# Degree counts in one run, routing between the gathers, and a rebuilt edge stage and combination in a graph and expert kernel

## The reference, cut to what matters

```python
# 1. relational graph layer
h_all = einsum('nd,rdo->rno', LN(x), W_r)                     # 16 products of every node
deg   = maximum(zeros((16, N)).at[edge_type, dst].add(1), 1)  # edges by relation and destination
msg   = h_all[edge_type, src] / deg[edge_type, dst][:, None]
x     = x + segment_sum(msg, dst) + LN(x) @ W0.T + b0
# 2. eight experts of F = 1024, one for each token, with a capacity
probs = softmax(LN(x) @ gate_w + gate_b); idx = argmax(probs); prb = the chosen probability
pos   = running count of the tokens of that expert - 1;  kept = pos < CAP
buf[idx, pos] = LN(x);  ybuf = relu(buf @ w1 + b1) @ w2 + b2  # each expert
x     = x + nan_to_num(ybuf[idx, pos] * prb * kept, nan=0, posinf=1e4, neginf=-1e4)
# 3. graph convolution with 1/sqrt(degree) at both ends, over the same edges and loops
# 4. an LSTM over the nodes and two running sums
```

## Time and profile before

| | |
|---|---|
| median of three runs | 4495.27 us |
| profiled execution | 4494.84 us, span 4493.1 us |
| granted TensorE clock, mean | 0.879 |
| TensorE busy | 3700.8 us (82%) |
| VectorE busy | 1837.3 us (41%) |
| ScalarE busy | 887.5 us (20%) |
| GpSimd busy | 1631.3 us (36%) |

### The profile page before, as it was taken

How to read it: one execution, slowest core, us unless ns; L and a number is a source line. 1 busy time by engine, 2 the same in 40 slices (tenths; PEclk the granted TensorE clock), 3 DMA queues, 4 the chain that set the end, 5 groups by cost and what they waited for, 6 DMA issues and landing times. The chain is left out here.

```text
span 4493.1 us, 64320 instructions
## 1 busy us (share of the span) xinstructions
PE 3700.8 (82%) x19849; PEld 2830.6 (63%) x19850; DVE 1837.3 (41%) x5512; ACT 887.5 (20%) x2492; POOL 1631.3 (36%) x1753
## 2 busy tenths in 40 slices
PE   3999999988878888865999865656667778999996
PEld 1444454457777777754666644555555557999996
DVE  3444420024334443444222283233344554444687
ACT  0333323310000000023111170000000002444453
POOL 1000000047777777733000036777777770000000
PEclk9999999978787777755999986788888899999998
DMA  4333333333333333332122054344455554433333
GB/s 156 121 120 123 125 116 149 147 117 111 110 110 111 111 111 110 111 122 90 62 82 80 28 158 133 107 126 136 148 152 161 174 183 156 148 111 115 108 108 107
DMA packets 213227, 545.38 MB, mean 121 GB/s; under 512 B 42897, under 2 KB 111358, under 8 KB 198119
## 3 DMA queue, kind: packets, MB, share of 16 engines
q1 hardware_dynamic: 121816, 297.98, 19.7%
q0 software_dynamic: 83344, 235.38, 17.8%
q10 hardware_dynamic: 7808, 8.92, 0.6%
HBM read 363.19 MB, written 178.51 MB: 121 GB/s over the span
## 5 line engine op out<-in xcount | busy, mean ns | idle before, releaser
L731 POOL DMA_INDIRECT a_msg<-scratch_hrel,k_rel_row x784 | 749.7, 956 | 1078.8 <-issue 1072.4
L1519 POOL DMA_INDIRECT b_msg<-scratch_gtab,k_src_row x784 | 763.2, 973 | 269.3 <-issue 263.5
L1568 PE MATMUL b_ps<-b_hit,b_msg 128*128 128x128 f32 x3136 | 492.6, 323 | 304.6 <-DMA b_msg<-scratch_gtab,k_src_row 296.4
L665 PE MATMUL r_psm<-k_w,r_xnT 128*128 128x512 f32 x1568 | 741.6, 609 | 0.9 <-ACT r_xnT L608 0.9
L834 PE MATMUL a_ps<-a_hit,a_msg 128*128 128x128 f32 x3136 | 562.9, 354 | 184.1 <-DMA a_msg<-scratch_hrel,k_rel_row 176.5
L1568 PEld LDWEIGHTS b_ps<-b_hit,b_msg 128*128 128x128 f32 x3136 | 460.9, 233 | 367.2 <-issue 299.6
L834 PEld LDWEIGHTS a_ps<-a_hit,a_msg 128*128 128x128 f32 x3136 | 522.2, 260 | 218.2 <-DVE a_hit L773 141.4
L1946 PE MATMUL l_psg<-k_hall,k_whhT 128*128 128x128 f32 x4672 | 565.8, 279 | 5.7 <-DVE k_hall L2063 5.5
L1946 PEld LDWEIGHTS l_psg<-k_hall,k_whhT 128*128 128x128 f32 x4672 | 542.9, 192 | 13.5 <-DVE k_hall L2063 5.9
L665 PEld LDWEIGHTS r_psm<-k_w,r_xnT 128*128 128x128 f32 x1568 | 278.0, 191 | 273.8 <-issue 251.8
L617 ACT COPY r_hst<-r_psm 128x512 f32<-128x512 f32 x392 | 229.6, 586 | 517.7 <-PE r_psm L665 517.5
(11 more groups left out here) (255 smaller groups left out, 3769.9 us busy)
## 6 DMA issues: line engine op xcount, KB each, us to landing
scratch_hrel<-r_hst SPq DMA_DIRECT2D x98, 1024.0 KB
l_xr<-scratch_xrow SPq DMA_DIRECT2D x146, 512.0 KB, 3.6
scratch_xrow<-n_xs SPq DMA_DIRECT2D x50, 512.0 KB, 3.2
a_msg<-scratch_hrel,k_rel_row POOLq DMA_INDIRECT x784, 2.8
b_msg<-scratch_gtab,k_src_row POOLq DMA_INDIRECT x784, 2.8
scratch_buf<-k_zpad POOLq DMA_DIRECT2D x8, 1024.0 KB, 6.6
scratch_ybuf<-x_ys POOLq DMA_DIRECT2D x8, 1024.0 KB
x_xr<-scratch_buf SPq DMA_DIRECT2D x7, 1024.0 KB, 15.1
```

The source lines that it names most:

```text
L665: mm = pe.matmul(psm[:, c % 4], xnT[:, u, kk], k.w[:, kk, c * 512:(c + 1) * 512], start=(kk == 0), stop=(kk == 1))
L731: pool.indirect_dma_start(msg[:, q, j], None, table, bass.IndirectOffsetOnAxis(ap=rows[:, g, j:j + 1].bitcast(U32), axis=0)).then_inc(s_m[ ...
L1519: pool.indirect_dma_start(msg[:, q, j], None, k.gtab, bass.IndirectOffsetOnAxis(ap=k.src_row[:, g, j:j + 1].bitcast(U32), axis=0)).then_in ...
L1568: mm = pe.matmul(ps[:, u, kk, 0:WIN], msg[:, g % SL, j, kk * P:(kk + 1) * P], hit[:, u, j], start=(j == 0), stop=(j == PER - 1))
```

## The change

The edge stage loads rows 0 to 95 and the 97th row apart, gives each of the three arrays a semaphore, takes W_r's loads behind them on the same queue, lets ScalarE load W0, the bias and the first four tiles of x, turns W0 there, and shares the evictions and memsets out. `Degrees` has buffers for seven groups, and all seven are counted behind chunk 7; the row sums are ten products of the spread counts with a selector of five columns, before the last tile. Gathers and routing become one stage, written out in full as the second gather stage is, with tile work set between groups from the group at which a tile is finished. Tokens are routed in batches of 8 (five), 6 and 3. The gate is written as column 256 of a row of `buf`, which is 264 wide. The experts weigh, clamp and test their outputs themselves and load their first weights at their start. The combination only gathers and adds, with eight and four buffers in place of six and three, and VectorE normalises every even tile.

```diff
@@ class Degrees
-        self.hit = sb("d_hit", [P, 2, PER, WIN], BF16)
+        self.hit = sb("d_hit", [P, BUNCH, PER, WIN], BF16)      # BUNCH = 7, CUTS = 5
+        self.n = k.NP // CUTS
+        self.wide, self.inv = (sb(n, [CUTS * k.R, self.n], F32) for n in ("d_wide", "d_inv"))
+        self.sel = sb("d_sel", [P, 2, CUTS], F32)
@@ count
         pe.wait_ge(self.s_p, 2 * g + 2)
-        pe.wait_ge(self.s_add, g + 1)
+        pe.wait_ge(self.s_add, g - u + BUNCH)
         for j in range(PER):
-            mm = pe.matmul(self.ps[0:self.k.R, u, 0:WIN], self.hot[:, u, j], self.hit[:, u, j],
+            mm = pe.matmul(self.counted(u), self.hot[:, u, j], self.hit[:, u, j],
@@ rows_pe
-        for t in range(k.NP // P):
-            mm = pe.matmul(self.ps[:, 0, t:t + 1], k.degT[:, t * P:(t + 1) * P], k.ones[0:k.R, 0:1],
+        pe.wait_ge(self.s_sel, 3)
+        pe.wait_ge(self.s_go, 16 * CUTS)
+        for t in range(self.n // P):
+            mm = pe.matmul(self.ps[:, 0, t * CUTS:(t + 1) * CUTS], self.wide[:, t * P:(t + 1) * P],
+                           self.sel[0:CUTS * k.R, 1], start=True, stop=True)
@@ stage_relations, vector, counting tiles
-                                for c in range(PT):
-                                    g = (XR * i + s) * PT + c
-                                    q = s * PT + c
-                                    deg.build(v, g + 1, (q + 1) % 2)
-                                    deg.add(v, g, q % 2, None)
+                                adds(XR * i + s)
+                                builds(XR * i + s + 1)
@@ scalar: the root of tile t + 2
-                        if more >= 2:
-                            ln.root(act, t + 2)
...
+                            if c == 6 and more >= 2:
+                                ln.root(act, t + 2)
@@ tensor
                             if c == 3 and more:
                                 turn(t + 1, 1 - u)
-                            if c < len(groups):
-                                deg.count(pe, *groups[c])
+                        for g in groups:
+                            deg.count(pe, *g)
...
-                    if counted:
-                        deg.rows_pe(pe, NG + 2)
                     with pe.Fori(LB, NB) as i:
...
+                    if counted:
+                        deg.rows_pe(pe)
                     tile(NR - 1, 0, False, [])
@@ stage_edges, sync
-                sp.wait_ge(s_fill, 3)
                 for a, v in enumerate((dst, src, etype)):
                     rows = v[0:full * EG].rearrange("(g e) -> g e", e=EG)
-                    sp.dma_start(raw[:, a, 0], rows[0:H]).then_inc(s_ld, 16)
-                    sp.dma_start(raw[0:full - H, a, 1], rows[H:full]).then_inc(s_ld, 16)
+                    sp.dma_start(raw[:, a, 0], rows[0:H]).then_inc(s_ld[a], 16)
+                    sp.dma_start(raw[0:low, a, 1], rows[H:H + low]).then_inc(s_ld[a], 16)   # low = 96
+                    if a == 0:
+                        sp.wait_ge(s_tail, 2)
+                    sp.dma_start(raw[low:full - H, a, 1], rows[H + low:full]).then_inc(s_ld[a], 16)
...
+                    if a == 0:
+                        ...                      # firsts -> base_i, with a semaphore of its own
+                for r in range(k.R):
+                    sp.dma_start(k.w[:, :, r * k.D:(r + 1) * k.D],
+                                 W_r[r].rearrange("(k p) o -> p k o", p=P)).then_inc(k.s_w, 16)
@@ stage_first (in place of stage_gather, weighted, and stage_route), gpsimd
+                    for g in slots:
+                        if along and g < NG:
+                            q = g % SL
+                            if g >= SL:
+                                hold(k, pool, s_mm, g - SL + 1)
+                            for j in range(PER):
+                                pool.indirect_dma_start(msg[:, q, j], None, table, ...).then_inc(s_m[q][j], 16)
+                        for b in ended(g - 10):
+                            scatter(b)
@@ tensor
+                    for g in slots:
+                        if along and g + 1 < NG:
+                            weigh(g + 1)
+                        if along and g < NG:
+                            sums(g)
+                        for t in begun(g - 4):
+                            logits(t)
+                        for b in ended(g - 6):
+                            ranks(b)
+                        for t in begun(g - 3):
+                            turn(t)
+                        for t in begun(g):
+                            turn_sums(t)
@@ scalar
+                    for g in slots:
+                        for b in ended(g - 5):
+                            powers(b)
+                        for t in begun(g - 3):
+                            turn(t)
+                        for t in begun(g - 2):
+                            norm(t)
+                        for t in begun(g - 1):
+                            root(t)
@@ vector
+                    for g in slots:
+                        if along and g + 2 < NG:
+                            hot(g + 2)
+                        if along and g + 1 < NG:
+                            build(g + 1)
+                        for b in ended(g - 7):
+                            route_slots(b)       # writes the gate into column D of xn
+                        for b in ended(g - 6):
+                            route_choice(b)
+                        for b in ended(g - 5):
+                            route_logits(b)
+                        for t in begun(g - 2):
+                            scale(t)
+                        for t in begun(g - 1):
+                            rows(t)
+                        if along and g < NG:
+                            add(g)
+        for_windows(k, "a_", scan, ended=lambda: tiles(False), fixed=lambda: tiles(True), flag=k.late)
@@ stage_experts
-                        sp.wait_ge(S["tp"], TB * (e - 1))
+                        sp.wait_ge(S["yg"], TB * (e - 1))
                     sp.dma_start(xr[:, u], rows(e)).then_inc(s_x[u], 16)
@@ scalar
+                weights(act, 0)
+                weights(act, 1)
...
+                    for n in range(TB):
+                        t = TB * e + n
+                        act.wait_ge(S["yt"], t + 1)
+                        if t >= 2:
+                            act.wait_ge(S["yc"], t - 1)
+                        act.activation(yg[:, n % 2], y[:, n % 2], ACT.Copy, scale=xr[:, e % 2, n, D:D + 1]).then_inc(S["yg"], 1)
@@ vector: finish(t), one block behind
+                    v.tensor_scalar(ys[:, n], yg[:, n % 2], 10000.0, -10000.0, ALU.min, ALU.max).then_inc(S["m"], 1)
+                    v.tensor_scalar(fin[:], yg[:, n % 2], 0.0, 0.0, ALU.mult, ALU.is_equal).then_inc(S["m"], 1)
+                    v.wait_ge(S["m"], 2 * t + 2)
+                    v.copy_predicated(ys[:, n], fin[:], yg[:, n % 2]).then_inc(S["yc"], 1)
@@ stage_combine
-    YR, XR = 6, 3
+    YR, XR = 8, 4
...
-                    v.tensor_scalar(yc[:, u], ys[:, u], 10000.0, -10000.0, ALU.min, ALU.max).then_inc(S["c"], 1)
-                    v.tensor_scalar(fin[:, u], ys[:, u], 0.0, 0.0, ALU.mult, ALU.is_equal).then_inc(S["f"], 1)
...
-                    v.copy_predicated(yc[:, u], fin[:, u], ys[:, u]).then_inc(S["p"], 1)
...
+                    if u == 0:
+                        if t >= 2:
+                            v.wait_ge(S["tp"], t - 1)
+                        v.tensor_scalar(xn[:, 0], xo[:, t % XR], mv[:, u, 0:1], rstd[:, u, 1:2], ALU.subtract, ALU.mult
+                                        ).then_inc(s_n[0], 1)
```

997 lines of the change are left out of this document (531 added, 466 removed).

## The result

The changed kernel took 4293.04 us, median of four runs (4287.72 to 4296.36), against 4495.69 for the kernel before on the same chip: ratio 0.9547, 95% interval 0.9530 to 0.9563. Forecast was 4315 with a range of 4280 to 4368. The profiled execution took 4290.27 (span 4287.7), 204.6 less than before's 4494.84; the sum of the forecast was 179. In the table a minus is time saved; the forecasts for the relations are those for the counts and for the row sums.

The account below looks back on a forecast made before the run. Five limits by stage: load waits, relation matmuls, row sums, GpSimd's gathers, then routing after them. Gains 39 + 32 + 17.5 + 80 − 4.5 + 15 = 179 from 4494.84 give 4315 us; own range 4300 to 4335, with rivals 4280 to 4368.

Parts of the forecast that it names:

- rival B: Whole kernel: everything cheap, counting run at 1.89 us, gathers at 1.261, combination gaining 17; gain 207, 4288 us; chance 0.13.
- Edges: Edge stage: faster loads and shared evictions bring the first relation product to 45 us; gain 39, bounds 25 and 45.
- Counts: Relation stage: seven count groups in one run of 28 cost 2.5 us a tile, not 3.66; gain 32, bounds 0 and 50.
- the lower end by the single-count rows: Relation stage: run of 28 counts at 0.057 us apart plus 0.29 for switching costs 1.89 us; gain 50.
- Rival A: Relations and combination: register waits keep the run at 3.66 us, low clock holds combination's gain to 5; 4357 us; chance 0.15.
- Row sums: Relation stage: 100 records, 20.5 us of TensorE, become 20 records before the last tile, 3 us; gain 17.5.
- "hidden" for the reciprocal: Relation stage: about 8 us of reciprocal on the spread counts runs beside TensorE at no cost; without cover 4 us.
- Gathers with routing: First gather stage: routing between gathers, 1.27 us pace, GpSimd stays the bound; gain 80, bounds 49 and 96.
- Rival C: Merged gather stage: VectorE locks GpSimd out, each DMA takes 1.485 us, stage grows by 177; 4492 us; chance 0.03.
- Rival D: Merged gather stage: hand-offs in fixed order bind it at 7.0 us a slot, losing 243; 4639 us; chance 0.05.
- Experts: Expert stage: later weight loads cost 2.5 us, the last block's weighing, clamp and test 2.0; cost 4.5, bounds 2 and 10.
- Combination: Combination stage: less VectorE and ScalarE work brings the mean slot from 2.396 to 2.08 us; gain 15, bounds 5 and 20.

Follow-up runs that it names:

- four edits: Changed kernel with degT's memset after the third cast, one norm before the reciprocal, fewer expert weights fetched first, combination's turning before the product: 4276.46 us, ratio 0.9509.

## Why the prediction came out right

The time lies within the range stated, but above all because the range took in rival B; the forecast's own range, 4300 to 4335, was missed. The stages run one after the other, so each term is checked by its stage's time. Runs that undo a part exist for the counts and for the merging; for edges, row sums, experts and combination the account rests on the two traces and on the small edits.

**Edges**, 42.3 for 39. The loads of 96 rows took the 12.22 us out of the queue, as said. `e_base_i` issued at 6.52 was used by 13.80 at the latest, not 17.5, but VectorE's start was not the only thing: its first cast was held up for 4 us beside the memset that the prediction had placed on GpSimd as free. By the four edits, that cost the end of the stage 0.4 us, by all runs some 1 us. The Trainium skill ("DMA: Bandwidth & Descriptors", Why a DMA increments its semaphore by 16 and not by 1) lets such a load run on the largest number of engines up to sixteen that divides its row count, which for 97 rows is one. The DMA share of 0.07 at 24 GB/s in the earlier trace rows agrees with one in sixteen. For the cast, the Trainium skill ("SBUF — State Buffer", Who interferes with whom) says that a cast can take the port pair it shares with GpSimd, and that whoever comes second is blocked for the whole instruction of the first. The 4.73 us against 0.68, ending with the memset, agree.

**Counts**, 28 × 1.80 = 50.4 for 32. The term was mis-sized: 2.5 us was taken for a run, with 0.3 for each group's register waits, and it is 1.86, where the lower end by the single-count rows was 1.89. The waits between the groups cost nothing that shows: 28 products in seven groups are 0.056 apart throughout. Rival A's ground, a run that stays at 3.66, is refuted. The Trainium skill ("TensorE: Matmul & The Clock Gate", Back-to-back issue gap) gives about 81 ns to each pair of such a stream at 128 columns. The traces differ, and they decide: 0.056 us, with weights of 16 and of 128 columns.

**Row sums**, 63.5 − 50.4 = 13.1 for 17.5. The 20 records cost 2.3 us, where 3 was priced. What failed is "hidden" for the reciprocal (8.15 us long, 8 in the prediction). The prediction looked for its cover in SyncE's stores; what stood behind it was the norm for which ScalarE's root waits. It cost 4.35 us, near the 4 that the prediction had for an uncovered one. Before, the row sums had cost a little more than the 20.5 counted, for the sixteen products behind them took 10.00 us where sixteen otherwise take 7.03:
```profile
622.75 10.00 PE L665 MATMUL r_psm<-k_w,r_xnT 128*128 128x512 f32 x16
```
18.3 + 3.0 − 2.3 − 4.35 = 14.6; where the other 1.5 went was not traced.

**Gathers with routing**, 84.0 for 80. Pace 1.265 for 1.27; tail 40.4 with its stage switch for 38.2. By the run with routing behind, 73 to 74 of it is the merging. Rival C does not hold: the gathers' mean is 959 ns beside VectorE's routing and 956 to 962 without. Rival D's mechanism, hand-offs in fixed order that hold a queue, was not there on the chip of the forecast and is there where gathers land late, some 90 us of GpSimd's queue, a price that took the gain away but not more. The reason against it, that the second stage holds its pace with like pieces, doesn't cover scatters: they alone stand in the gathers' queue. So that the term of 80 held is in part luck with the chip: on the chip where before takes 4870 the merging gave nothing, and no row ahead of the forecast told of it.

**Experts**, 7.5 for 4.5, within 2 to 10. The load that is late is not w1's but the rows': the second block of `x_xr` was there at 1930.48, 3.5 us after the first, beside 4 MB of weights for two experts, issued from 1924.44 to 1928.7. From the loads to the first `x_psh` it is 13.1 us where it was 7.8, so 5.3 for the 2.5 that was priced; the other 2.2 are the weighing of the last block, priced 2.0. Taking away all but 1 MB of the weights at first gave back 2.3.

**Combination**, 22.6 for 15 and above the bound of 20. The mean slot came out as priced, (2500.3 − 2401.2) / 48 = 2.065 for 2.08, with TensorE at either clock. What was missed is what stands ahead of the loop: the first product comes 7.0 us after the first `c_yr`, and came 11.5 after it (2588.1 less 2576.6). ScalarE's table load of 1.28 us stood in that stretch before and lies ahead of the first `c_yr` now, and the weighing, clamp and test are gone from it. Before's mean slot, measured from the first product to the last, was (2704.5 − 2588.1) / 48 = 2.425, not 2.396. 4.5 + 48 × 0.36 = 21.8.

The total, 205 for 179, is the sum of these: counts +18, combination +8, gathers +4, edges +3, against row sums −4 and experts −3. It lies beside rival B (4288), whose run at 1.89 held; its gathers at 1.261 did not.

## What to carry to other kernels

Small products that share an engine with large ones are cheapest in one run with one entry; where its buffer is single, place it last in the loop, so that what fills the buffer has the whole of the next turn. In a queue in program order, place the instruction that depends on another engine as far behind as the queue's own lead can grow, not where it stood ready in one trace: with a lead of seven groups and slots made seven behind, ten was too few, and that cost nothing on one chip and about 60 us on others. Time an overlap on more than one chip before its gain is believed.

## What was not expected of the hardware

- The same program differs by 8 to 9% between chips (4497 and 4870 to 4902 us), nearly all of it in the stages with indirect gathers (in the kernel with four edits 1087 against 1366, and 1040 against 1202), though issuing one of the first gather stage takes the same 0.96 us. Relations, experts and LSTM agree within 4 us, at the same granted clock (1.00 in the relations on both chips). What holds the gather stages there stays open; the traces have no landing times on those chips, so that gathers land late is inferred from waits.
- A VectorE cast took 4.73 us beside a GpSimd memset of 16 × 6400, and 0.69 with the memset moved away; another, of 0.25 us, took 1.29 beside the moved memset.
- Between the edge stage and the next lie 6.8 to 7.9 us on VectorE in which nothing the profile shows is awaited, in every run of a changed kernel but one (4.9). What they wait for was not found.
- 28 bf16 products of 128 columns run 0.056 us apart at a granted clock of 1.00, with weights of 16 or of 128 columns.
